# Chunks of four tiles instead of two in the gather-and-scatter ring of a fused graph and mixture kernel

## The chip, the cores and the metric

One core of one Trainium2 chip runs the whole program. The time is the device time of one execution in microseconds; three runs of the kernel before gave a median of 10040.12 us. A profile is one further execution, recorded by the hardware profiler.

## What is computed

Cut to what matters (the dense branches in words):

```python
edge_index = jnp.stack([src, dst])          # 206250 edges, sorted by dst, 6250 nodes, D = 256
xn = layernorm(x)                           # (6250, 256) float32
h = xn
for l in range(3):                          # three relational graph layers, 8 relations
    agg = segment_sum(h[src], edge_type * 6250 + dst).reshape(8, 6250, 256)
    y = einsum('rnd,rde->ne', agg, W[l]) + h @ root[l] + bias[l]
    h = relu(y) if l < 2 else sigmoid(y)
x = x + h + mix(xn)                         # 8 heads of linear attention and a 1024-wide MLP
x = x + moe(layernorm(x))                   # 8 experts, top 2
```

All tensors are float32.

## The kernel before, in words

The order of sum and product is turned round. For each layer, each node's vector is first multiplied with all eight relation matrices and the root matrix; the nine results are a row of a table in HBM (`table[l]`, 56250 rows of 256 floats). The sum over edges is then a gather of table rows and a sum into the node of `dst`. Nodes are taken in 50 **windows** of 125 (`WIN`).

**Phases.** Phase 0 normalises x and fills the first table. Phases 1, 2 and 3 each do a layer's sum window by window, and lay other dense work between two windows: phase 1 the products for the next table and the attention's projections, phase 2 the products for the third table, attention output and MLP, phase 3 router and experts. Between phases all tables must be stored.

**Tiles, chunks, units.** The edges lie in tiles of 128 (`TILE`). `TILES` tiles are a chunk (2 before), `UNIT` chunks are a unit (2, so four tiles), and `RING` chunks (13) are the ring in SBUF, and also a body, the length of the loops on POOL and SP. There are 62 bodies, 806 chunks, 403 units, 1612 tiles. The count of edges is rounded up to whole bodies; pad tiles have index 0 and a target that matches no node. For each window a first and last unit come from a table of bounds that the kernel computes from `dst` (lines 783 to 805). The unit at a window's border is read by both windows; the last window runs to the last unit.

**POOL** (lines 432 to 449): for each chunk it waits until its slot is free (`slots_free`, L443), and issues one indirect DMA a tile (L447): 128 rows of 1 KB from the table, by 128 indices in `idx_now`. Each adds 16 to `gathered[s]`. Twice a body, at slots 0 and `GROUP_A` (7), it waits for the reload of the indices (L441).

**SP** (lines 372 to 382): it waits for each chunk to have landed, in order, adds 1 to `chunks_ready` (L378), and reloads the indices of a group of chunks when all of it has landed (L380).

**DVE** (`onehot_unit`, L842 to L853): for each chunk it waits until the one-hot buffer's last use is over (`onehot_used`, L848), and makes the one-hot matrices of all tiles of the chunk in one instruction (L849): target of the edge against the 125 nodes of the window. There are two buffers, so a one-hot can be made once the matmuls of the chunk before the last are complete. `first_onehots` (L855) makes the first two of the next window ahead.

**PE** (`scatter`, L1151 to L1184): for each chunk it waits for `chunks_ready` and `onehot_ready`, and does one matmul a tile (L1169), which the trace records as two: one-hot (128 x 125) times gathered rows (128 x 256), added up in `ps_out`. The last one of a chunk adds 1 to `onehot_used` on completion. After every unit but a window's first it waits until all units before this one are complete and then frees `UNIT` chunks (L1179, L1180): the slots are freed one unit late, since the border unit is read again. At the window's end L1183 adds the root term and signals `out_done`. ACT then makes `h_win` (L599, L654, L698 in the three phases), PE transposes it (L1108), ACT copies it out (L483), and the products (L1130) follow. In phase 3 PE goes on with the router (L1334) and the experts (L1344, L1355) of the window before.

Of the kernel before, what the change touches and what calls it, by code (L numbers as in the profile page):

```python
# [26 lines left out]
WIN = 125  # L27
WIN_A = 112
TILE = 128
TILES = 2  # L30
RING = 13
UNIT = 2
GROUP_A = 7


def gps_program(nc, t):
# [6 lines left out]
    assert nodes % WIN == 0 and NW % 2 == 0  # L43
    body_edges = TILE * TILES * RING
    BODIES = -(-edges // body_edges)
    CHUNKS = BODIES * RING
    while CHUNKS % UNIT:
        BODIES += 1
        CHUNKS += RING
    UNITS = CHUNKS // UNIT  # L50
    NT = CHUNKS * TILES
    TB = -(-NT // 128)
# [20 lines left out]
    with ExitStack() as ctx:  # L73
        ctx.enter_context(nc.allow_non_contiguous_dma(reason="a few vectors go to a feature a partition"))

        def sb(name, shape, dt=FP32):
            return ctx.enter_context(nc.sbuf_tensor(name, shape, dt))
# [15 lines left out]
        targets = sb("targets", [128, TB * 128])  # L93
        idx_now = sb("idx_now", [128, RING * TILES], U32)
        ring = sb("ring", [128, RING * TILES * D])
        onehot = [sb(f"onehot{i}", [128, TILES, WIN]) for i in range(UNIT)]
        nodes_now = sb("nodes_now", [128, WIN])
# [78 lines left out]
        ordC = edges // SP_  # L176
        assert 3 * ordC <= RING * TILES * D
        order_a = ring[:, 0:ordC].bitcast(I32)
# [154 lines left out]
        def _(sp):  # L333
# [30 lines left out]
            sp.wait_ge(prep_ev, 2 * TB)  # L364
            groups = ((0, GROUP_A), (GROUP_A, RING))
            for g, (s0, s1) in enumerate(groups):
# [22 lines left out]
        def _(pool):  # L389
# [42 lines left out]
            for l in range(3):  # L432
# [3 lines left out]
                with pool.Fori(0, layer_turns) as i:  # L436
                    turn = pool.snap(layer_turns * l + i)
                    for s in range(RING):
                        if s in (0, GROUP_A):

                            pool.wait_ge(idx_loaded[int(s == GROUP_A)], turn * 16 + 16)  # L441

# [961 lines left out]
```

## Time and profile before

| | |
|---|---|
| median of 3 runs | 10040.12 us (10038.99 to 10089.25) |
| profiled execution, span | 10274.9 us |
| its own time beside the span | not recorded; the span is taken for it |
| busy: PE, PE weight load | 6298.0 us (61%), 4307.1 us (42%) |
| busy: POOL, DVE, ACT | 4692.1 us (46%), 2244.8 us (22%), 1095.0 us (11%) |
| DMA | 899.6 MB, mean 88 GB/s |

Engines: PE is TensorE's matmuls, PEld its weight loads, DVE is VectorE, ACT ScalarE, POOL GpSimd, SP SyncE. L849 is line 849 of the kernel. "idle before" is time in which the engine stood still before these instructions; after the arrow stands what ended it. "issue" is a wait that nothing in the profile explains, "remote" and "another core or an unknown queue" one that ended with a semaphore's change to which the profile finds no instruction. PEq and DVEq are the engines' sequencers. The ends of matmuls are modelled from their size, not observed.

### The profile page before, as it was taken

The page shows a single profiled execution, that of the slowest core. Times are in us where ns is not written, and L with a number is a line of the kernel's source. Part 1 is how long each engine was busy: PE and PEld are TensorE (multiplying, and loading weights), DVE is VectorE, ACT ScalarE, POOL GpSimd, SP SyncE. Part 2 cuts the span into 40 slices and gives each one's busy share as a digit, 9 for nine tenths or more (in the row PEclk, how much of TensorE's full clock was granted, in tenths as well). Part 3 has the DMA queues.
Part 4 walks back from the last instruction along what each step waited for, and adds up shares of the span by engine and source line. Part 5 has one row for each costly group of instructions (what it writes and reads, how often), then busy time and mean ns, then how long its engine had stood idle before and what let it go on. Part 6 is the DMA issues. An engine that isn't in the chain of part 4 may idle for free.

```text
span 10274.9 us, 106460 instructions
## 1 busy us (share of the span) xinstructions
PE 6298.0 (61%) x23187; PEld 4307.1 (42%) x23188; DVE 2244.8 (22%) x6475; ACT 1095.0 (11%) x2855; POOL 4692.1 (46%) x4958
## 2 busy tenths in 40 slices
PE   5866556555556666666666665664666665556666
PEld 2333333333333334444444444443444444444445
DVE  2311111111111122222222221222222222222222
ACT  1110000000000000000000000010111111111111
POOL 0134555554555544444444444445444444444443
PEclk9977777777777777777777777777777777777777
DMA  4443333333333333333332323323222222222222
GB/s 120 131 123 95 93 93 98 99 94 93 95 93 96 97 89 89 92 91 91 90 91 87 90 87 93 89 86 97 67 73 67 69 68 71 72 70 69 67 68 60
DMA packets 410721, 899.60 MB, mean 88 GB/s; under 512 B 149828, under 2 KB 236588, under 8 KB 391946
## 3 DMA queue, kind: packets, MB, share of 16 engines
q0 software_dynamic: 232128, 634.17, 21.4%
q10 hardware_dynamic: 116050, 257.82, 8.2%
q1 hardware_dynamic: 62518, 7.30, 0.6%
q8 instruction: 12, 0.20, 0.0%
q14 instruction: 13, 0.11, 0.0%
HBM read 704.42 MB, written 192.01 MB: 87 GB/s over the span
## 4 chain that ended last, share of the span: by engine, by line
PE 38%; issue 29%; another core or an unknown queue 27%; DVE 2%; ACT 2%; ACTq 1%; DVEq 1%; DMA 1%; POOL 0%; POOLq 0%; SPq 0%; PEld 0%; PEldq 0%
PE ps_out L1169 17%; PE ps_y L1130 8%; PE ps_y L1344 3%; PE ps_tr L1286 2%; PE ps_b L1355 2%; PE ps_c L1355 2%; DVE onehot L849 1%; PE ps_tr L1108 0%; PE ps_out L1183 0%; ACT L713 0%; DVEq L849 0%; PE ps_b L1274 0%; PE ps_c L1230 0%; DVEq L885 0%
## 5 line engine op out<-in xcount | busy, mean ns | idle before, releaser
L447 POOL DMA_INDIRECT ring<-table,idx_now x4836 | 4634.1, 958 | 4979.6 <-PEq L1180 3530.7
L1169 PE MATMUL ps_out<-ring,onehot 128*125 x10848 | 3342.2, 461 | 2881.1 <-issue 1772.5
L1169 PEld LDWEIGHTS ps_out<-ring,onehot 128*125 128x125 f32 x10848 | 2290.8, 225 | 3938.9 <-issue 3574.5
L849 DVE TENSOR_TENSOR onehot<-targets,nodes_now 128x250 f32<-128x250 f32 x2712 | 1131.5, 422 | 5341.1 <-remote 2955.1
L1130 PE MATMUL ps_y<-W,hT 128*125 128x512 f32 (+1 forms) x3000 | 1347.1, 600 | 17.5 <-DVE y_stage L739 16.4
L1130 PEld LDWEIGHTS ps_y<-W,hT 128*125 128x125 f32 x3000 | 598.9, 207 | 606.7 <-issue 560.5
L1344 PEld LDWEIGHTS ps_y<-hT,big 128*128 128x128 f32 x3200 | 440.2, 207 | 25.4 <-issue 4.7
L1355 PE MATMUL ps_b<-big,gT 128*125 128x256 f32 x800 | 268.1, 467 | 294.6 <-ACT gT L713 282.2
L1344 PE MATMUL ps_y<-hT,big 128*128 128x125 f32 x3200 | 444.5, 291 | 5.5 <-issue 5.4
L462 ACT COPY y_stage<-ps_y 125x512 f32<-125x512 f32 x450 | 263.5, 585 | 1002.0 <-PE ps_y L1130 973.3
L1286 PE MATMUL ps_tr<-W,gT 128*125 128x256 f32 x800 | 258.2, 493 | 94.6 <-ACT gT L663 94.6
L426 POOL TENSOR_TENSOR rstd<-mv,neg_half 125x1 f32<-125x1 f32 x100 | 54.8, 548 | 554.0 <-DVE mv L822 478.7
L1355 PEld LDWEIGHTS ps_b<-big,gT 128*125 128x125 f32 x800 | 164.3, 229 | 341.8 <-ACT gT L713 291.7
L713 ACT ACTIVATE gT<-ps_y,b1e 128x125 f32<-128x125 f32 x800 | 236.7, 364 | 544.5 <-PE ps_y L1344 343.3
L1286 PEld LDWEIGHTS ps_tr<-W,gT 128*125 128x125 f32 x800 | 196.6, 252 | 165.5 <-ACT gT L663 121.2
L599 ACT ACTIVATE h_win<-ps_out 125x256 f32<-125x256 f32 x50 | 19.2, 383 | 2115.3 <-remote 959.5
L739 DVE COPY y_stage<-ps_y 125x512 f32<-125x512 f32 x150 | 103.7, 691 | 614.4 <-PE ps_y L1130 542.3
L654 ACT ACTIVATE h_win<-ps_out 125x256 f32<-125x256 f32 x50 | 19.2, 383 | 1986.3 <-issue 856.5
L698 ACT ACTIVATE h_win<-ps_out 125x256 f32<-125x256 f32 x50 | 19.2, 383 | 1970.0 <-PE ps_out L1183 941.6
L1355 PE MATMUL ps_c<-big,gT 128*125 128x256 f32 x800 | 200.6, 384 | 0.2 <-ACT gT L713 0.2
L1108 PE MATMUL ps_tr<-ident,h_win 125*128 125x125 f32 x200 | 47.1, 320 | 215.8 <-issue 94.6
L1049 DVE SCALAR_TENSOR_TENSOR acc<-ps_b,combine,acc 125x256 f32<-125x256 f32 x200 | 96.8, 484 | 316.9 <-PE ps_b L1355 313.2
(172 smaller groups left out, 2819.1 us busy)
## 6 DMA issues: line engine op xcount, KB each, us to landing
table<-y_stage ACTq DMA_DIRECT2D x150, 1008.0 KB
ring<-table,idx_now POOLq DMA_INDIRECT x4836
base_in<-table ACTq DMA_DIRECT2D x150, 125.0 KB
table<-y_stage ACTq DMA_DIRECT2D x150, 117.0 KB
x_in<-in_x_dram ACTq DMA_DIRECT2D x100, 125.0 KB
xn_in<-xn_scratch ACTq DMA_DIRECT2D x100, 125.0 KB
xn_scratch<-xn_in ACTq DMA_DIRECT2D x50, 125.0 KB
res_scratch<-res_win ACTq DMA_DIRECT2D x50, 125.0 KB
```

The source lines that it names most:

```text
L426: nc.gpsimd.tensor_tensor(rstd[:, :], mv[:, 1:2], neg_half[:, :], ALU.pow).then_inc(rstd_ready, 1)
L447: nc.gpsimd.indirect_dma_start(ring[:, c * D:(c + 1) * D], None, table[l], bass.IndirectOffsetOnAxis(ap=idx_now[:, c:c + 1], axis=0)).then ...
L462: nc.scalar.copy(y_stage[parity][:, b * 2 * D:(b + 1) * 2 * D], ps_y[BANK[b]][0:WIN, 0:2 * D]).then_inc(y_evac_act, 1)
L713: last = nc.scalar.activation(gT[:, (e % GB) * K + f, :], ps_y[e % 3][:, f * WIN:(f + 1) * WIN], ACT.Gelu, bias=b1e[:, e, f:f + 1])
L739: nc.vector.tensor_copy(y_stage[parity][:, 2 * D:4 * D], ps_y[1][0:WIN, 0:2 * D]).then_inc(y_evac_dve, 1)
L849: nc.vector.tensor_tensor(onehot[u][:, :, :], targets[:, bass.ds(col + u * TILES, TILES)].unsqueeze(2).broadcast_to([128, TILES, WIN]), no ...
L1049: nc.vector.scalar_tensor_tensor(out=acc[parity][:, :], in0=(ps_b, ps_c)[e // 2 % 2][0:WIN, e % 2 * D:(e % 2 + 1) * D], scalar=combine[:, ...
L1130: last = nc.tensor.matmul(ps_y[BANK[b]][0:WIN, 0:n], hT[parity][:, k, :], W[:, k, b * 2 * D:b * 2 * D + n], start=(k == 0), stop=(k == K - 1))
L1169: mm = nc.tensor.matmul(ps_out[0:WIN, 0:D], onehot[u][:, j, :], ring[:, bass.ds(slot + j * D, D)], start=(start and u == 0 and j == 0), st ...
L1286: last = nc.tensor.matmul(ps_tr[0:WIN, 0:D], gT[:, j, :], W2[:, j, :], start=(j == 0), stop=(j == FJ - 1))
L1344: last = nc.tensor.matmul(ps_y[e % 3][:, f * WIN:(f + 1) * WIN], w1e[:, e, k, f * 128:(f + 1) * 128], hT[parity][:, k, :], start=(k == 0), ...
L1355: last = nc.tensor.matmul((ps_b, ps_c)[e // 2 % 2][0:WIN, e % 2 * D:(e % 2 + 1) * D], gT[:, (e % GB) * K + f, :], w2e[:, e, f, :], start=( ...
```

## The change

Four tiles make a chunk and eight a unit; the ring holds six chunks (24 tiles instead of 26), reloaded in two groups of three. All counts that hang on these constants follow: a one-hot instruction makes 128 x 500 elements, a body has 24 tiles, and bodies, chunks, units and pad tiles are counted anew. No other line changes.

```diff
-TILES = 2
-RING = 13
+TILES = 4
+RING = 6
 UNIT = 2
-GROUP_A = 7
+GROUP_A = 3
```

## Rows read from the trace of the kernel before

**Rows 1.** The page: the chain by engine, and two of the costliest groups.
```profile
PE 38%; issue 29%; another core or an unknown queue 27%; DVE 2%; ACT 2%; ACTq 1%; DVEq 1%; DMA 1%; POOL 0%; POOLq 0%; SPq 0%; PEld 0%; PEldq 0%
...
L447 POOL DMA_INDIRECT ring<-table,idx_now x4836 | 4634.1, 958 | 4979.6 <-PEq L1180 3530.7
...
L849 DVE TENSOR_TENSOR onehot<-targets,nodes_now 128x250 f32<-128x250 f32 x2712 | 1131.5, 422 | 5341.1 <-remote 2955.1
```

**Rows 2.** Line L1183 in the three phases: durations, first and last start.
```profile
L1183 PE MATMUL ps_out<-base_in,ident x100: 377/380/451, 710.4 to 3604.8; 125*125 125x256 f32 x100
...
L1183 PE MATMUL ps_out<-base_in,ident x100: 377/381/634, 3717.5 to 6918.8; 125*125 125x256 f32 x100
...
L1183 PE MATMUL ps_out<-base_in,ident x100: 376/381/635, 7014.8 to 10236.4; 125*125 125x256 f32 x100
```

**Rows 3.** Timeline of a window of phase 1: start, duration, what, idle before.
```profile
2022.17 11.01 PE L1169 MATMUL ps_out<-ring,onehot 128*125 x44
...
2026.00 0.95 POOL L447 DMA_INDIRECT ring<-table,idx_now  x1 [12.15 <-PEq L1180]
...
2035.64 0.42 DVE L849 TENSOR_TENSOR onehot<-targets,nodes_now 128x250 f32<-128x250 f32 x1 [3.84 <-remote]
...
2049.90 0.94 POOL L447 DMA_INDIRECT ring<-table,idx_now  x1 [0.30 <-issue]
2054.17 0.42 DVE L849 TENSOR_TENSOR onehot<-targets,nodes_now 128x250 f32<-128x250 f32 x1 [9.54 <-remote]
```

**Rows 4.** The chain in the same window, and into the next: start, duration, what.
```profile
2031.44 3.94 another core or an unknown queue
...
2036.10 7.92 another core or an unknown queue
...
2044.28 9.63 another core or an unknown queue
...
2061.64 0.43 PE ps_out L1183 x2
...
2064.11 0.43 PE ps_tr L1108 x2
...
2080.15 10.66 PE ps_out L1169 x40
```

**Rows 5.** Stretches of 2 us: PE, PEld, DVE, ACT, POOL, PEclk, DMA share, GB/s.
```profile
2018.00:2020.00 2.00, 2.00 (x9) 1.28 (x8) 0.65 (x2) 0.37 (x1) 0.00 (x0) 1.00 0.00 0
...
2052.00:2054.00 2.00, 0.00 (x0) 0.00 (x0) 0.00 (x0) 0.00 (x0) 0.00 (x0) 0.50 0.08 15
```

**Rows 6.** Timeline after that window's scatter, ACT.
```profile
2063.67 0.38 ACT L599 ACTIVATE h_win<-ps_out 125x256 f32<-125x256 f32 x1 [40.72 <-remote]
...
2066.54 0.37 ACT L483 COPY hT<-ps_tr 128x250 f32<-128x250 f32 x1 [2.49 <-remote]
```

**Rows 7.** A window's end in phase 3: first the chain, then the timeline.
```profile
7122.69 13.96 another core or an unknown queue
...
7147.71 0.87 PE ps_c L1355 x4
...
7154.84 1.85 PE ps_out L1169 x8
...
7134.89 0.95 POOL L447 DMA_INDIRECT ring<-table,idx_now  x1 [0.30 <-issue]
...
7138.90 1.39 ACT L713 ACTIVATE gT<-ps_y,b1e 128x125 f32<-128x125 f32 x5 [0.36 <-remote]
```

**Rows 8.** The chain between two scatters of phase 2: first and last piece.
```profile
5214.33 0.43 PE ps_out L1183 x2
...
5235.98 3.45 PE ps_y L1130 x8
```

**Rows 9.** Timeline at the start of the first gathers.
```profile
636.99 1.18 POOL L447 DMA_INDIRECT ring<-table,idx_now  x1 [24.09 <-issue]
...
647.14 0.80 ACT L580 ACTIVATE xhatT<-ps_a,cols 128x125 f32<-128x125 f32 x2 [0.77 <-PE ps_a L1211]
```

## The prediction

> **What bounds the kernel now.** I read the page first. Its chain charges TensorE with 38% of the span, "issue" with 29% and "another core or an unknown queue" with 27% on a one-core program [rows 1]: over half the path is waiting. The gathers (L447) are busy 4634 us and idle 4980 us, mostly until PE frees slots (L1180); they bound nothing on the average. The one-hots (L849) are busy 1132 us. Next, where the time lies: the closing matmul of a window (L1183) comes 50 times a layer, at a mean distance of 59.1, 65.3 and 65.7 us (first to last over 49) [rows 2]. So 9315 of 10275 us are 150 windows of two parts, the scatter (L1169 over about 18 chunks) and the dense work.
>
> Then one window of the first layer. The scatter begins at 2022.17 and does 11 chunks (44 matmul records) in 11.01 us. The POOL had stood still for 12.15 us with the ring full; at 2026.00 slots come free and it gathers without pause, 20 gathers 1.25 us apart, the last at 2049.90 [rows 3]. Six microseconds into this burst the scatter nearly stops: the chain shows waits of 3.94, 7.92 and 9.63 us, each ended by a one-hot, with one chunk between two [rows 4]. The data is not late: between 2018 and 2020 the DMA engines moved 0 GB/s, so the chunks that follow in the ring had landed [rows 5]. The one-hot is not slow: 0.42 us. It starts late, as DVE itself idled 3.84 us until a "remote" event [rows 3], and in the loop DVE waits for one thing, `onehot_used`, which a matmul increments. Those matmuls were recorded long before. My reading: **a PE completion signal, immediate otherwise, is late while a long run of gathers is under way**, by 2 us at first and 8 to 10 us later, and all come through some 3.3 us after the last gather (burst over at 2050.84, next one-hot at 2054.17) [rows 3]. It isn't only the ring's matmuls: L1183 ends at 2062.07 and ACT reads its result at 2063.67, 1.6 us later; the transposes behind it end at 2064.54 and ACT copies at 2066.54 [rows 4, 6]. In layer 3 a chain of such waits lasts 13.96 us, until 7136.65, just after the last gather of that burst (7134.89), and the first gelu follows at 7138.9 [rows 7].
>
> So two cycles meet in a window: PE, free for 10 us, empties the ring; then it stands until the 25 us burst is over.
>
> **The change, part by part.**
> Counts. A body holds 6 x 4 x 128 = 3072 edges; 206250 need 68 bodies, 408 chunks, 204 units, 1632 tiles instead of 1612. A unit is visited once, and once more at each window's border: 204 + 49 = 253 visits of 8 tiles, 2024 a layer instead of 452 x 4 = 1808.
> (1) One-hots: 2712 become 1518, each twice as large. Of 422 ns [rows 1], between the same 422 and double, 844; I take 0.68 us. Beside eight matmuls it is hidden either way; if it weren't, 1518 x 0.68 = 1.03 ms is less than the 1.13 ms now.
> (2) Matmuls: the handshake (one-hot, signal, four matmuls, signal) paces PE at 1.0 us per two tiles [rows 3]. With eight per chunk it should fall back to the bare 0.217 us (four of equal width take 0.87 [rows 7]), 1.73 us for four tiles. A window's 40.5 tiles would need 17.5 us instead of 18.1 for 36.2: the extra tiles are paid by the rhythm. Taken as 0; between -0.6 and +2.2 us a window.
> (3) Prefetch: slots are freed one unit late (the unit at the border is read again). Of 26 tiles in the ring 22 lie ahead of a window's start now; of 24, 16 will.
> (4) SP and POOL: waits, increments and POOL's slot waits halve in number. idx reloads: groups of 12 gathers (15 us) each instead of 14 and 12. Nothing on the path; the 3-chunk group still gives 15 us of cover to a reload.
> (5) Pad tiles: 20 more gathers a layer, all in the last window, which runs to the last unit: 20 x 1.25 = 25 us, 75 us in all. Bound: 0 if hidden.
>
> Now a window, from its first ring matmul. PE does chunks 0 to 3 without waiting; at the fourth's start (5.2 us) it frees the border unit. Now the fourth chunk starts at 3.0 us (11 chunks in 11.01) and POOL's first gather 0.8 later, at 3.83 [rows 3]; so it will be 6.0. The second unit is freed 3.5 us later, the third when chunk 7's data is there: 8 gathers, 6.0 + 7 x 1.25 + 3 = 17.8 us, before the 16 gathers freed so far are spent (26.0). The landing time of 3 us is from the last gather at 2049.90 and traffic that has died down to 15 GB/s by 2052 to 2054 [rows 3, 5]. The fourth unit is freed when chunk 9 can start: its data is there at 6.0 + 15 x 1.25 + 3 = 27.8 us, and it needs chunk 7's completion signal (matmuls done at 20 to 21, late by 4 to 8 us: 24 to 29). Both come before 36.0, the end of the granted gathers. **So the burst does not break**: 1612 / 50 = 32.2 gathers in one run, 40.3 us, over at 46.3. PE's last ring matmul is done at about 32, but its signals stand behind two or three others that pass at 8 to 10 us each; L1183's comes with the end of the burst, 46.3 + 3.3 = 49.6 us.
> From there the dense work runs clear of gathers. Layer 1: from ACT's read at 2063.67 to the next ring matmul at 2080.15 are 16.5 us, less the 2.0 of the late transpose signal: 14.5 [rows 4, 6]. Layer 3: from 7138.9 to 7154.84, 15.9 [rows 7]. Layer 2: 5214.76 to 5239.43 are 24.7 us with late signals inside; between 14.5 and 24.7, I take 19.5, as its up-projection and gelus wait within [rows 8].
> Windows: 64.1, 69.1, 65.5 us against 59.1, 65.3, 65.7: +5.0, +3.8, -0.2, in sum 8.6, x 49 = +421 us. With the pads **+496 us**. The profiled execution spans 10274.9, the median of the runs is 10040.1, 2.3% less; I carry the difference over in microseconds: about 10540 us.
>
> The Trainium skill (SBUF - State Buffer, "SBUF: two separate sides") says that the engines' and the DMA's ports are disjoint and neither can slow the other. By that rule gathers couldn't hold up TensorE's completions; the trace disagrees in its 3.94, 7.92 and 9.63 us waits, unless their cause is another (rival A). The same notes (TensorE: Matmul & The Clock Gate, "The cost: per-tile semaphore tail") price an increment at 26.3 ns; by that alone 1194 fewer would give 31 us, an estimate by that page, and the time would be 10084 with the pads.
>
> **Rivals.**
> A, signals on time (11%): if what makes them late is the number of handshakes, it goes with half of them. Then the scatter is paced by gathers, 32.5 us; windows of 47, 52 and 48.4, -42.7 x 49 + 75: 8025 us. Against: lateness shows on signals of the dense work as well [rows 6, 7].
> B, signals late by some 5 us each, however long the burst (16%): L1183's passes at about 41 us; windows 55.5, 60.5, 56.9: -17.2 x 49 + 75 = -770, 9270 us. This is the case of the **other side**: it decides at chunk 9, and wins if L1183's signal arrives before 46 us on the mean (three windows of h + dense work 14.5, 19.5 and 15.9 against 190.1, less 1.5 for the pads). For: in the run's first burst, begun at 636.99, a transpose signal at 647.1 was not late at all [rows 9]. Against: in the burst shown each wait is longer than the one before it [rows 4].
> C, the burst breaks (14%): if chunk 7's signal comes after 36.0 us, POOL runs dry, signals clear at about 40, and a second short burst covers the dense work as now. h at 43.5: 60, 65.5, and 69.7 in layer 3, whose up-projections wait for the second burst: +5.1 x 49 + 75, 10365 us.
> D, worse (8%): layer 2's dense work keeps its 24.7 us and 16.5 stay in layer 1: 66.5, 74.7, 68: 11050 us.
> E, no change (6%): prefetch lost and rhythm gained cancel. A rival that the change does nothing it says I rule out: all loops take TILES and RING.
>
> **The numbers.** The forecast, 45%, is 10540; its own range is 10350 to 10900. Faster, A and B: 0.27. Within 0.5% (about what a measurement of this kernel can tell): 0.06. Slower, forecast, C and D: 0.67. The range of 9250 to 10900 holds the forecast, B, C and E, 81%.
>
> **What would show it.** POOL: one run of 32 to 40 gathers a window instead of 20 and 12, idle 4.98 ms about as now. L1169: about 0.22 us per matmul while free. ACT at h_win: its idle time up, ended 3 us after the last gather of each burst. L1183 some 32 us after the window's first ring matmul, h_win at 49.6. Distances of L1183 of 64.1, 69.1, 65.5. I am wrong in the reading itself if signals arrive at once in the middle of a 40 us burst, and wrong in size if h_win starts well before the burst's end.

## The result, and the profile after

The kernel after takes 10958.61 us (median of 4 runs, 10948.59 to 10959.58), the kernel before, beside it, 10052.5 us (10038.99 to 10089.25): a ratio of 1.0895, 95% interval 1.0873 to 1.0917. That is 906 us slower; the forecast was 10540 us, and its range ended at 10900.

The page of the kernel after: the span, the chain by engine, and the groups that answer to [rows 1].

```profile
span 10957.3 us, 97403 instructions
...
another core or an unknown queue 57%; PE 22%; issue 13%; ACT 3%; ACTq 2%; PEld 1%; DVE 1%; DMA 1%; POOL 0%; PEldq 0%; DVEq 0%; POOLq 0%; SPq 0%
...
L447 POOL DMA_INDIRECT ring<-table,idx_now x4896 | 4735.5, 967 | 5566.7 <-PEq L1180 4101.7
L1169 PE MATMUL ps_out<-ring,onehot 128*125 x12144 | 3429.5, 444 | 1549.4 <-issue 741.7
...
L849 DVE TENSOR_TENSOR onehot<-targets,nodes_now 128x500 f32<-128x500 f32 x1518 | 1032.6, 683 | 5450.1 <-remote 2178.9
...
L599 ACT ACTIVATE h_win<-ps_out 125x256 f32<-125x256 f32 x50 | 19.2, 383 | 2483.8 <-remote 2135.1
```

No engine has enough new work to explain 906 us: the gathers cost 101 us more, the scatter's matmuls 87 us more for 12% more records, the one-hots 99 us less. What grew is waiting. The share of the chain that no instruction accounts for went from 27% to 57%, and ACT's idle time before `h_win` in the 50 windows of phase 1 is 2484 us, 2135 of them ended by a "remote" event. In the kernel before these two were 2115 and 960 us:

```profile
L599 ACT ACTIVATE h_win<-ps_out 125x256 f32<-125x256 f32 x50 | 19.2, 383 | 2115.3 <-remote 959.5
```

The closing matmul of a window in the three phases, as in [rows 2]:

```profile
L1183 PE MATMUL ps_out<-base_in,ident x100: 377/381/634, 688.6 to 3931.5; 125*125 125x256 f32 x100
...
L1183 PE MATMUL ps_out<-base_in,ident x100: 377/382/634, 4033.0 to 7464.5; 125*125 125x256 f32 x100
...
L1183 PE MATMUL ps_out<-base_in,ident x100: 377/381/634, 7544.2 to 10918.8; 125*125 125x256 f32 x100
```

First to last over 49: 66.2, 70.0 and 68.9 us, against 59.1, 65.3 and 65.7. By the starts in these rows the three times 49 distances sum to 10049 us against 9317, 732 us more. Outside them some 50 us fell away, so the spans differ by 682 us.

One window of phase 1, as in [rows 3]. Timeline: start, duration, what, in brackets the idle time before it.

```profile
2021.94 10.52 PE L1169 MATMUL ps_out<-ring,onehot 128*125 x48
...
2027.96 1.02 POOL L447 DMA_INDIRECT ring<-table,idx_now  x1 [25.37 <-PEq L1180]
...
2037.00 0.75 DVE L849 TENSOR_TENSOR onehot<-targets,nodes_now 128x500 f32<-128x500 f32 x1 [3.59 <-PE ps_out L1169]
...
2043.03 0.68 DVE L849 TENSOR_TENSOR onehot<-targets,nodes_now 128x500 f32<-128x500 f32 x1 [5.28 <-issue]
...
2053.10 1.06 PE L1183 MATMUL ps_out<-base_in,ident 125*125 125x256 f32 x2
...
2057.19 0.68 DVE L849 TENSOR_TENSOR onehot<-targets,nodes_now 128x500 f32<-128x500 f32 x1 [12.52 <-remote]
...
2067.74 0.95 POOL L447 DMA_INDIRECT ring<-table,idx_now  x1 [0.30 <-issue]
2073.34 0.38 ACT L599 ACTIVATE h_win<-ps_out 125x256 f32<-125x256 f32 x1 [50.62 <-remote]
2073.43 0.68 DVE L849 TENSOR_TENSOR onehot<-targets,nodes_now 128x500 f32<-128x500 f32 x1 [15.55 <-remote]
```

POOL restarts 6.02 us after the first ring matmul and issues 32 gathers without a gap, until 2068.69. The closing matmul is over at 2054.16. ACT, which waits for nothing but its signal, starts at 2073.34: **19.2 us after the matmul, and 4.65 us after the end of the last gather's instruction.** The window is no exception: over the 50 windows of each phase `h_win` starts 20.4, 19.1 and 20.5 us behind the matmul in the median (0.75, 0.04 and 0.04 us in the kernel before), and 5.1 us behind the last gather. The chain of the same stretch consists of little else:

```profile
2018.67 3.45 PE ps_y L1130 x8
...
2023.84 49.48 another core or an unknown queue
2073.34 0.39 ACT h_win L599
```

### The profile page after: what moved, and what is told of

Read it like the earlier page. It is cut to its first block, busy times and chain, and to the rows that moved or that the text cites. A ratio compares the mean times of both kernels' runs of the same rounds, so it can differ in the third digit from the quotient of the medians.

```text
span 10957.3 us, 97403 instructions
## 1 busy us (share of the span) xinstructions
PE 6489.4 (59%) x24483; PEld 4714.6 (43%) x24484; DVE 2141.2 (20%) x5281; ACT 1095.9 (10%) x2855; POOL 4793.5 (44%) x5018
## 4 chain that ended last, share of the span: by engine, by line
another core or an unknown queue 57%; PE 22%; issue 13%; ACT 3%; ACTq 2%; PEld 1%; DVE 1%; DMA 1%; POOL 0%; PEldq 0%; DVEq 0%; POOLq 0%; SPq 0%
PE ps_y L1130 7%; PE ps_out L1169 3%; PE ps_y L1344 2%; PE ps_b L1355 2%; PE ps_c L1355 2%; PE ps_tr L1286 1%; PE ps_b L1274 1%; PE ps_c L1274 1%; PEld ps_out L1169 1%; ACTq L472 1%; PE ps_tr L1108 1%; ACT L713 1%; ACT y_stage L462 0%; ACTq L669 0%
## 5 line engine op out<-in xcount | busy, mean ns | idle before, releaser
L447 POOL DMA_INDIRECT ring<-table,idx_now x4896 | 4735.5, 967 | 5566.7 <-PEq L1180 4101.7
L1169 PE MATMUL ps_out<-ring,onehot 128*125 x12144 | 3429.5, 444 | 1549.4 <-issue 741.7
L1169 PEld LDWEIGHTS ps_out<-ring,onehot 128*125 128x125 f32 x12144 | 2611.0, 220 | 2363.6 <-issue 1917.3
L849 DVE TENSOR_TENSOR onehot<-targets,nodes_now 128x500 f32<-128x500 f32 x1518 | 1032.6, 683 | 5450.1 <-remote 2178.9
L1108 PE MATMUL ps_tr<-ident,h_win 125*128 125x125 f32 x200 | 65.5, 428 | 1695.0 <-ACT h_win L599 840.7
L1344 PE MATMUL ps_y<-hT,big 128*128 128x125 f32 x3200 | 516.1, 299 | 576.0 <-issue 575.5
L1108 PEld LDWEIGHTS ps_tr<-ident,h_win 125*128 125x128 f32 x200 | 28.1, 198 | 1745.9 <-ACT h_win L599 864.1
L1344 PEld LDWEIGHTS ps_y<-hT,big 128*128 128x128 f32 x3200 | 485.5, 215 | 599.0 <-issue 578.0
L599 ACT ACTIVATE h_win<-ps_out 125x256 f32<-125x256 f32 x50 | 19.2, 383 | 2483.8 <-remote 2135.1
L654 ACT ACTIVATE h_win<-ps_out 125x256 f32<-125x256 f32 x50 | 19.2, 383 | 2331.8 <-remote 2053.6
L698 ACT ACTIVATE h_win<-ps_out 125x256 f32<-125x256 f32 x50 | 19.2, 383 | 2319.8 <-remote 2046.6
L1286 PE MATMUL ps_tr<-W,gT 128*125 128x256 f32 x800 | 194.6, 397 | 27.7 <-ACT gT L663 27.7
```

What stands on the lines that cost most here:

```text
L447: nc.gpsimd.indirect_dma_start(ring[:, c * D:(c + 1) * D], None, table[l], bass.IndirectOffsetOnAxis(ap=idx_now[:, c:c + 1], axis=0)).then ...
L849: nc.vector.tensor_tensor(onehot[u][:, :, :], targets[:, bass.ds(col + u * TILES, TILES)].unsqueeze(2).broadcast_to([128, TILES, WIN]), no ...
L1108: last = nc.tensor.transpose(ps_tr[:, k * WIN:(k + 1) * WIN], src[:, k * 128:(k + 1) * 128], ident[0:WIN, 0:WIN])
L1169: mm = nc.tensor.matmul(ps_out[0:WIN, 0:D], onehot[u][:, j, :], ring[:, bass.ds(slot + j * D, D)], start=(start and u == 0 and j == 0), st ...
L1286: last = nc.tensor.matmul(ps_tr[0:WIN, 0:D], gT[:, j, :], W2[:, j, :], start=(j == 0), stop=(j == FJ - 1))
L1344: last = nc.tensor.matmul(ps_y[e % 3][:, f * WIN:(f + 1) * WIN], w1e[:, e, k, f * 128:(f + 1) * 128], hT[parity][:, k, :], start=(k == 0), ...
```

## The experiments

All are compared with the kernel before on the same chip. Each of the five sets ran on another chip, and these turned out to be of two kinds. (No chip was used for two sets, so whether the kind belongs to the chip or to its state at that time was not seen; the chip of the result and that of the profile of the kernel before are not recorded.) On three (sets 1, 4 and 5) the kernel before took 10047 to 10228 us, as in the result above; on two (sets 2 and 3) it took 6879 and 6876 us. I call the first kind "holding", the second "prompt", for what their traces show of PE's signals. The expectations of sets 1 and 2 were written when only the holding kind was known. "Theory G" in them is the prediction's mechanism: PE's completion signals are held back as long as a run of gathers lasts.

### Set 1, holding (before 10082.0 us): which part of the change, and two rivals to the cause

**Unit of eight tiles alone, chunks of two.**

```diff
-RING = 13
-UNIT = 2
-GROUP_A = 7
+RING = 12
+UNIT = 4
+GROUP_A = 6
```

> The change with its unit but not its chunk: TILES 2, UNIT 4, RING 12, GROUP_A 6, so chunks of two tiles, units of eight, 24 tiles in the ring, four one-hot buffers. Theory G (completion signals of PE are late while a run of gathers lasts, and eight-tile releases let the run last until all gathers of a window are done): as slow as the change, runs of 32 gathers, h_win some 5 us after a run's end, 10850 to 11050 us. Rival S (what counts is how many signals there are per tile): twice the change's signals, so the run breaks or the scatter stops as in the kernel before, 10000 to 10400 us.

Measured 10246.25 us, ratio 1.017 (1.0134 to 1.0207), in rival S's range and not in theory G's. In its trace most runs of gathers break after 24, and `h_win` starts some 44 us into the window.

**Chunk of four alone, unit of one chunk (four tiles), and so a single one-hot buffer.**

```diff
-TILES = 2
-RING = 13
-UNIT = 2
-GROUP_A = 7
+TILES = 4
+RING = 6
+UNIT = 1
+GROUP_A = 3
```

> The change with its chunk but not its unit: TILES 4, UNIT 1, RING 6, so one signal and one one-hot per four tiles, and slots freed by four tiles; there is one one-hot buffer only, so PE pauses about 1 us at each chunk. Theory G: the run of gathers breaks again in most windows, because a late signal holds back the next release sooner; between 9900 and 10600 us. Rival S: halving the signals is what cost the time, so 10900 us or more.

Measured 10504.05 us, ratio 1.0426 (1.0375 to 1.0476); runs again break, mostly after 20 to 24. This lies in theory G's range and not in S's. So neither half makes the 906 us, and neither theory foresaw both results. My reading, which no run tests by itself: only both together leave few enough signals, each worth enough tiles, for a run to last all 32 gathers.

**A shallow queue of gathers.** From the third slot of the ring on POOL waits until the chunk before the last has landed, so that at most two chunks, four gathers, are under way.

```diff
                         apart(pool)
+                        if s >= 2:
+                            pool.wait_ge(gathered[s - 2], (turn + 1) * (16 * TILES))
+                            apart(pool)
```

> The kernel before, but POOL waits before a chunk's gathers until the chunk before the last has landed (not for the first two slots of a body), so at most four gathers are under way or queued, without a pause between gathers. Theory G: it is the run of gathers itself that makes signals late; same time within 1%, waits of 4, 8 and 10 us in each window as before. Rival Q (signals are late while gathers are queued up on POOL, and the granted ones are dispatched far ahead): signals on time, scatter at the rate of gathers, 7300 to 8600 us.

Measured 10055.94 us, ratio 0.9977 (0.9954 to 1.0). The wait leaves nine in ten gathers without a gap (4401 of 4835 follow within 0.35 us, 4504 in the kernel before), and the time stays: it is not the depth of POOL's queue.

**No reads of the ring.** The scatter multiplies with a constant tile (the sum over edges is left out).

```diff
-                                                  ring[:, bass.ds(slot + j * D, D)],
+                                                  Wx[:, 0, :],
```

> The kernel before, but the scatter's matmuls read a constant tile (part of Wx) in place of the gathered rows, so the sum over edges is left out; all waits, gathers and signals stay. Theory G: signals as late as before, 9900 to 10200 us. Rival R (a matmul that reads the ring while gathers write into it is slow or acknowledged late): signals on time, 7300 to 8600 us.

Measured 10091.71 us, in one run, where the kernel before took 10031 to 10106. Reading what the gathers write is not the cause either.

### Set 2, prompt (before 6879.12 us)

**The kernel after, a gap once in 24 gathers.** POOL lets the chunk before land first, at slot 3 of 6.

```diff
                         apart(pool)
+                        if s in (3,):
+                            pool.wait_ge(gathered[s - 1], (turn + 1) * (16 * TILES))
+                            apart(pool)
```

> The kernel after, with one wait more on POOL: before the fourth chunk of each ring turn it waits for the third chunk to land, so that a run of gathers can hold 24 at most and has a gap of some 3 us behind it. Theory G (PE's completion signals are held back while a run of gathers lasts, and come at its end): the run breaks after at most 24 gathers instead of 32, h_win comes at some 44 us of the window instead of 51.3, and the time is 10100 to 10450 us, near the 10246 of chunks of two tiles with units of eight, although chunk size, unit and ring are those of the kernel after. Rival S (the time goes by the size of chunk and unit itself: waits for four one-hots at once, a ring of six): 10850 to 11150 us, since the extra waits can only cost. What tells: the trace's runs of gathers by length, and h_win's start after the window's first matmul.

**The same at slots 1, 3 and 5: runs of 8.**

> The kernel after, with such a wait before the second, fourth and sixth chunk of each ring turn: runs of 8 gathers (10 us), each with a gap of some 3 us behind it. Theory G: no signal is held longer than about 8 us, the scatter ends early (20 to 30 us of the window) and h_win starts within 5 us of it; POOL itself then needs 32 x 1.25 + 4 x 3 = 52 us a window, so the time is 8300 to 9600 us, below both kernels. Rival P (POOL becomes the bound: each gap costs more than 3 us, or work of the dense part is held back just as much): 10000 to 10900 us. Rival S: 11000 us or more.

**The kernel before, a quarter of each row's bytes** (sum over edges left out).

```diff
-                                ring[:, c * D:(c + 1) * D], None, table[l],
+                                ring[:, c * D:c * D + D // 4], None, table[l].rearrange("n (q d) -> (n q) d", q=4),
```

> The kernel before, where each gather brings a quarter of each row's bytes and the scatter reads a constant tile in place of the ring (the sum over edges is left out). The number of gathers, rows and waits is unchanged. Theory V (it is the bytes written to SBUF that hold the signals back): with a quarter of them the signals come on time and the time falls to 8000 to 9300 us. Theory N (it is the gathers themselves, their number and their rows, whatever bytes they bring): 10000 to 10120 us, no change from the 10082 us of the same kernel with full rows.

**The kernel after, each window's last release put off** until PE has `h_win` or the tanh.

```diff
                 unit(first, True)
-                    with pe.Fori(first + 1, last + 1) as pos:
+                    with pe.Fori(first + 1, last) as pos:
...
+                    n = unit(last, False)
+                    pe.wait_ge(onehot_used, n + UNIT)
...
+                    def release():
+                        apart(pe)
+                        with pe.If(last > start):
+                            pe.sem_inc(slots_free, UNIT)
```

> The kernel after, where PE releases the last two chunks of each window's scatter not when their matmuls are done but after it has h_win (layers 1 and 2) or the tanh (layer 3). Theory G: POOL runs out of free slots about 4 to 8 gathers earlier, so the run ends at some 36 to 41 us of the window instead of 46.2, the held signals come 5 us behind that, and h_win starts at 41 to 46 us instead of 51.3; the remaining gathers run beside the dense part. 147 windows x 5 to 8 us earlier, less what the later gathers cost the next scatter: 9900 to 10500 us. Rival L (the gathers put off are late for the next window, whose scatter waits for them): 10800 to 11300 us, with the gap moved from h_win to the first matmuls of the ring.

Measured, in this order: 8369.28 us, ratio 1.216 (1.214 to 1.218); 8925.08 us, 1.2976 (1.2955 to 1.2998); 6860.73 us, 0.9976 (0.9966 to 0.9986); 8130.96 us, 1.1815 (1.1795 to 1.1835). The second lies in theory G's range and the third speaks, by its number, for bytes as the cause. But the kernel before itself took 6879 us, and in all four traces `h_win` starts 0.04 us behind the closing matmul whatever the gathers do. So the set says nothing on what holds signals back; only the comparison beside each number kept this from becoming a false proof. The last edit was tried here alone (45 us slower than the kernel after on the other prompt chip); on a holding chip it wasn't tried.

### Set 3, prompt again (before 6875.69 us): what the change costs where no signal is late

> The kernel after itself, beside the kernel before. In the last set of runs the kernel before took 6879 us instead of 10050, and no completion signal of PE was late in any of four kernels (h_win 0.04 us behind the scatter's last matmul). Where the kernel before takes 6879 us, theory C (with signals on time the kernel before is bound by POOL's gathers, 41 us a window, and the change takes that away: a ring released 8 tiles at a time starves POOL): the kernel after takes 8000 to 8300 us (ratio 1.16 to 1.21), 47 to 51 us a window, h_win 0.04 us behind the scatter. Rival (the change is nearly free there, and the deferred release was what cost): 6900 to 7200 us. Where the kernel before takes 10050 us: 10900 to 11000 us again, ratio 1.08 to 1.10.

Measured 8086.43 us, ratio **1.176** (1.1739 to 1.1781). The window that answers to the one above:

```profile
2002.67 2.74 PE L1169 MATMUL ps_out<-ring,onehot 128*125 x8 [3.18 <-SPq L378]
...
2015.83 1.06 PE L1183 MATMUL ps_out<-base_in,ident 125*125 125x256 f32 x2
...
2016.93 0.38 ACT L599 ACTIVATE h_win<-ps_out 125x256 f32<-125x256 f32 x1 [31.60 <-PE ps_out L1183]
...
2030.99 10.52 PE L1169 MATMUL ps_out<-ring,onehot 128*125 x48
...
2036.91 1.12 POOL L447 DMA_INDIRECT ring<-table,idx_now  x1 [5.45 <-PEq L1180]
```

The same instructions at the same pace (first stretch of 48 records again 10.52 us), but `h_win` comes 0.04 us after the matmul instead of 19.2, while gathers are under way. The dense part ends at 2030.99, and POOL stands still for 5.45 us at the start of the window, until the border unit is read again and freed (over the whole run such a gap is 7.3 us in the median, once a window). The kernel before has no trace of its own on such a chip. In its trace with a quarter of the bytes that gap isn't there: it goes on at the pace of its gathers through the window's border, and so is bound by POOL:

```profile
1536.76 0.94 POOL L447 DMA_INDIRECT ring<-table,idx_now  x1 [0.30 <-issue]
...
1537.29 0.68 PE L1183 MATMUL ps_out<-base_in,ident 125*125 125x256 f32 x2
1538.01 0.94 POOL L447 DMA_INDIRECT ring<-table,idx_now  x1 [0.30 <-issue]
1538.01 0.38 ACT L599 ACTIVATE h_win<-ps_out 125x256 f32<-125x256 f32 x1 [23.45 <-PE ps_out L1183]
```

**Unit of eight, chunks of two, again.**

> Chunks of two tiles, units of four chunks (8 tiles), a ring of twelve. Where the kernel before takes 6879 us: theory C says that the unit of 8 tiles is what starves POOL, so this takes most of the loss, 7900 to 8300 us; a rival says that the ring of six big chunks does it (a gather waits for a whole slot of four tiles), and this takes 6900 to 7300 us. Where the kernel before takes 10050 us: 10200 to 10300 us again.

Measured 7808.98 us, ratio 1.1362 (1.1343 to 1.1381), a little below the first theory's range and far above the rival's. 933 of the 1211 us come with the unit, its ring of 24 tiles and its 20 pad tiles a layer, 277 with the larger chunk.

> The kernel after with a gap of some 3 us behind every 8 gathers. Where the kernel before takes 10050 us: theory G (PE's signals are held back while a run of gathers lasts) 8900 to 9600 us, below both kernels, h_win within 5 us of the scatter's last matmul; rival P (dense part or gaps cost as much): 10000 us or more. Where it takes 6879 us: 8900 to 8950 us again.

Measured 8920.83 us: on a prompt chip gaps only cost, 834 us here.

> The kernel before with a quarter of each gathered row's bytes and a constant in place of the ring (the sum over edges is left out). Where the kernel before takes 10050 us: theory V (the bytes written hold the signals back) 6850 to 8000 us; theory N (the number of gathers and rows does) 10000 to 10120 us. Where it takes 6879 us: 6850 to 6870 us again, bound by 4836 gathers at 1.27 us.

Measured 6861.21 us.

### Set 4, holding (before 10046.55 us): the run of gathers is what holds the signals

**The kernel before with gaps.** Runs of 8 to 10 gathers, then POOL waits for the last chunk to land.

```diff
                         apart(pool)
+                        if s in (4, 8, 12):
+                            pool.wait_ge(gathered[s - 1], (turn + 1) * (16 * TILES))
+                            apart(pool)
```

> The kernel before with a wait on POOL for the chunk before to land, at three of the 13 slots of the ring: runs of 8 to 10 gathers, each with a gap of some 3 us. Where the kernel before takes 10050 us: theory G (the run of gathers holds the signals back, a gap lets them go) 8000 to 9500 us, ratio under 0.95; rival H (signals are late for another reason, and the gaps only cost) 10100 to 11500 us. Where it takes 6877 us, bound by gathers: 41 us a window plus 3.6 gaps of 3 us is 52 us, so 8200 to 8600 us, ratio 1.19 to 1.25, by every theory.

Measured **8476.84 us, ratio 0.8442** (0.8423 to 0.8462). Three waits on POOL, which add no work and take none away, make the kernel 16% faster. Its lines stand 3 lower: L1186 is L1183, L602 is L599, L852 is L849, L450 is L447. First its page:

```profile
PE 34%; issue 29%; another core or an unknown queue 16%; POOL 8%; DMA 6%; DVE 3%; ACT 2%; ACTq 1%; DVEq 1%; POOLq 0%; PEld 0%; PEldq 0%; SPq 0%
...
L450 POOL DMA_INDIRECT ring<-table,idx_now x4836 | 4640.9, 960 | 3175.5 <-issue 1588.7
```

Then the timeline of one window:

```profile
1715.65 1.12 POOL L450 DMA_INDIRECT ring<-table,idx_now  x1 [0.30 <-issue]
...
1718.64 0.42 DVE L852 TENSOR_TENSOR onehot<-targets,nodes_now 128x250 f32<-128x250 f32 x1 [2.69 <-PE ps_out L1172]
...
1721.95 0.95 POOL L450 DMA_INDIRECT ring<-table,idx_now  x1 [5.18 <-DMA ring<-table,idx_now]
...
1748.04 0.60 PE L1186 MATMUL ps_out<-base_in,ident 125*125 125x256 f32 x2
1748.67 0.38 ACT L602 ACTIVATE h_win<-ps_out 125x256 f32<-125x256 f32 x1 [34.04 <-PE ps_out L1186]
1749.28 0.95 POOL L450 DMA_INDIRECT ring<-table,idx_now  x1 [2.50 <-DMA ring<-table,idx_now]
```

The gathers cost what they cost before (4641 us against 4634), POOL is idle 1804 us less, and `h_win` is prompt in 49 of 50 windows of phase 1. It isn't everywhere: in phases 2 and 3 it is late in 14 and 20 of 50 windows, by up to 5.9 us. The held share of the chain falls from 27% to 16%.

**Chunk of four, unit of four, again.**

> Chunks of four tiles, a unit of one chunk (four tiles), a ring of six. Where the kernel before takes 6877 us: the window's scatter touches 36 tiles instead of 40, 12 gathers behind POOL's restart instead of 16, so it ends some 5 us earlier than in the kernel after (27 instead of 32 us) and the dense part of 14 to 18 us follows: 41 to 46 us a window, and 7000 to 7500 us. Rival (the chunk of four itself starves POOL as much as the unit): 7800 us or more. Where it takes 10050 us: 10400 to 10600 us again.

Measured 10497.45 us, ratio 1.0452 (1.0429 to 1.0474). How the chunk of four alone does on a prompt chip was not seen.

**A quarter of the bytes, now where signals are held.**

> As before: a quarter of each row's bytes, the sum over edges left out. Where the kernel before takes 10050 us: bytes theory 6850 to 8000 us, number theory 10000 to 10120 us. Where it takes 6877 us: 6860 us again.

Measured 10061.57 us, in one run, where the kernel before took 10019 to 10060. The chain by engine on its page, and then the chain in order of time in one window:

```profile
PE 39%; issue 31%; another core or an unknown queue 23%; DVE 2%; ACT 2%; ACTq 1%; DVEq 1%; DMA 0%; POOL 0%; POOLq 0%; SPq 0%; PEld 0%
```

```profile
1908.73 6.30 another core or an unknown queue
1915.28 8.84 another core or an unknown queue
1924.85 8.40 another core or an unknown queue
```

A quarter of the bytes moves nothing: what holds the signals goes with the gather instructions and their rows by number, not with what they write. Which of the two it is, POOL's instructions or the rows on their way, no run separates.

### Set 5, holding (before 10227.85 us): how the cost goes with the length of the run

The kernel after was not run on this chip; its 10958.61 us are from the result.

> The kernel after with a gap behind every 8 gathers. Where the kernel before takes 10050 us: theory G says that the hold goes, so the time is near the 8920 us that this kernel takes where no signal is late, 8900 to 9300 us, some 1800 us under the kernel after; a theory by which chunk and unit size cost the 906 us by themselves gives 10000 us or more. Where the kernel before takes 6877 us: 8920 us a third time.

Measured 9429.98 us, ratio 0.9224 (0.9201 to 0.9248). 130 us above the range: in phases 2 and 3 the dense part still takes 22 us where it takes 18 and 15 on a prompt chip.

> The kernel after with one gap for each 24 gathers. Where the kernel before takes 10050 us, theory G: runs of 12 to 24 gathers in place of 32, h_win at 30 to 45 us of the window instead of 51.3, 9000 to 10500 us, between the runs of 8 and the unbroken 32. A theory without the run's length: 10900 us or more. Where the kernel before takes 6877 us: 8370 us again.

Measured 10799.48 us, ratio 1.0565 (1.0538 to 1.0592): above theory G's range, and just under the other's. The group of `h_win` in phase 1, on its page and on that of the kernel with runs of 8:

```profile
L602 ACT ACTIVATE h_win<-ps_out 125x256 f32<-125x256 f32 x50 | 19.2, 384 | 2203.9 <-remote 1381.7
```

```profile
L602 ACT ACTIVATE h_win<-ps_out 125x256 f32<-125x256 f32 x50 | 19.2, 384 | 1891.7 <-PE ps_out L1186 1891.7
```

The first of the two is the kernel with runs up to 24. With runs of 8, none of ACT's waiting in phase 1 ends with a "remote" event any more; with runs up to 24, 1382 us of it do.

**The kernel before, gaps at two slots: runs of 12 to 14.**

```diff
+                        if s in (6, 12):
```

> The kernel before with gaps at two of the 13 slots: runs of 12 to 14 gathers. POOL's own bound is 41 us + 2.5 x 2.6 us = 47.5 us a window (7650 us in all); signals can be held up to 12 x 1.25 = 15 us. Where the kernel before takes 10050 us: 8000 to 9300 us; below 8477 if POOL's bound decides, above it if the hold does. Where it takes 6877 us: 7600 to 8000 us, bound by POOL.

Measured 9475.9 us, ratio 0.9264 (0.924 to 0.9288), 176 us above the range: longer runs are held longer, and that costs more than the gaps they save. In its trace `h_win` comes 4.9 us behind the closing matmul in the median window of phase 1, by up to 12.6, and most of ACT's waiting for it ends with a "remote" event:

```profile
L602 ACT ACTIVATE h_win<-ps_out 125x256 f32<-125x256 f32 x50 | 19.2, 383 | 1643.6 <-remote 1238.2
```

Runs of 8 to 10 were the best tried. Shorter ones were not.

All kernels on both kinds of chip, medians in us:

| kernel | longest run of gathers | holding | prompt | difference |
|---|---|---|---|---|
| before (bytes cut to a quarter) | holding mostly 20 to 24, prompt unbroken | 10062 | 6861 | 3200 |
| before, whole | holding the same, prompt not traced | 10047 to 10228 | 6876, 6879 | 3170 to 3350 |
| after | 32 | 10959 | 8086 | 2872 |
| unit of eight, chunk of two | holding mostly 24, prompt 32 | 10246 | 7809 | 2437 |
| after, runs up to 24 | 24 | 10799 | 8369 | 2430 |
| after, runs of 8 | 8 | 9430 | 8921, 8925 | 505 to 509 |
| before, runs of 8 to 10 | 10 | 8477 | not run | |

## Why the prediction was wrong

The direction and the mechanism were right, and most times in the window; the size was not: 496 us forecast, 906 measured. Two steps failed above all. The excess of the profile's span over the median was carried over in microseconds, which is 224 of the 410 us missing. And the dense part of a window, put at 14.5, 19.5 and 15.9 us, took 15.7, 19.7 and 18.1, which is 176 us. A later `h_win` (76 us) and the first and last windows (60 us) add to it, and 125 us come off again, as shown below.

**The burst.** Forecast: POOL begins at 6.0 us, does not break, is over at 46.3. Measured: 6.0 and 46.2 to 46.8 us, one run of 32 gathers in 135 of some 150 windows. The argument that the fourth unit would be freed before the granted gathers were spent held. **The counts** held too: 1518 one-hots of 0.683 us against 0.68, 12144 matmul records (three layers of 2024, each recorded as two), the bare rhythm of 0.22 us, the closing matmul at 31.2 us in the window shown (30.2 in the median) where I said 32. That the prefetch falls to 16 tiles is seen in the restart at 6 us.

**"L1183's comes with the end of the burst, 46.3 + 3.3 = 49.6 us": right in kind, short in size.** `h_win` starts at 51.3 us in the median window of phase 1, 4.65 us behind the last gather in the window shown. I had taken 3.3 us from a one-hot of the kernel before, behind a run of 20 gathers; behind a run of 32 it is more. On the mean of all windows, prompt ones included, `h_win` comes at 50.5, 50.0 and 50.5 us.

**"From there the dense work runs clear of gathers": right, but not at full pace.** The way from `h_win` to the next ring matmul takes 15.7, 19.7 and 18.1 us on the mean, against my 14.5, 19.5 and 15.9. On a prompt chip the same three are 14.4, 18.3 and 15.4. Part of the difference is TensorE's clock: PE had stood still for 19 us, and the stretches after it show a granted clock of 0.50 until 2082, the lower of its two levels (1.2 of 2.4 GHz); the prompt kernel, whose rest was shorter, was granted 0.93, 0.64 and 0.79 in its first 9 us. The two transposes (L1108) take 0.68 us at the lower level and 0.44 in the prompt kernel. How much of the difference the clock makes wasn't measured by itself. Stretches as in [rows 5], first the kernel after, then the same kernel on the prompt chip:

```profile
2073.00:2076.00 3.00, 0.68 (x2) 0.29 (x2) 0.68 (x1) 1.02 (x3) 0.00 (x0) 0.50 0.05 3
...
2079.00:2082.00 3.00, 3.00 (x5) 1.01 (x4) 0.69 (x1) 0.00 (x0) 0.00 (x0) 0.50 0.00 0
2082.00:2090.00 8.00, 8.00 (x33) 5.14 (x32) 0.65 (x2) 2.75 (x6) 0.00 (x0) 0.99 0.00 0
```

```profile
2017.00:2020.00 3.00, 0.70 (x4) 0.47 (x5) 0.00 (x0) 1.28 (x3) 2.39 (x3) 0.93 0.31 87
2020.00:2023.00 3.00, 3.00 (x7) 1.39 (x6) 0.14 (x1) 0.80 (x2) 2.09 (x3) 0.64 0.58 191
2023.00:2026.00 3.00, 3.00 (x12) 1.56 (x11) 0.56 (x1) 0.59 (x1) 2.39 (x3) 0.79 0.35 97
```

I had read the dense part's length from windows where the engine had not just rested so long, and left the clock out of the sum. A part of it was in my 14.5 us unseen: in the window of [rows 3] the granted clock was 0.50 and 0.58 from 2067 to 2073.

**The pads, "75 us in all": the price was near, the comparison was not.** The last window of a phase runs to the last unit. In phase 1 its closing matmul comes 93.8 us after the one before; in the kernel before it was 45.1 us:

```profile
3837.46 1.06 PE L1183 MATMUL ps_out<-base_in,ident 125*125 125x256 f32 x2
...
3931.25 0.60 PE L1183 MATMUL ps_out<-base_in,ident 125*125 125x256 f32 x2
```

```profile
3559.52 0.60 PE L1183 MATMUL ps_out<-base_in,ident 125*125 125x256 f32 x2
...
3604.62 0.60 PE L1183 MATMUL ps_out<-base_in,ident 125*125 125x256 f32 x2
```

With the other two phases, 99.3 against 48.4 and 98.2 against 52.3, that makes 145 us. The last windows of the kernel after are 28 to 31 us longer than its others, on the holding and on the prompt chip alike, some 88 us for the 75 I had priced. What I had overlooked is the other side: in the kernel before the last windows are 14 to 17 us shorter than its others. Their last run is of 10 gathers only, as nothing is left to gather for a next window.

**"I carry the difference over in microseconds": this alone is 224 of the 410 us missing.** The profiled execution of the kernel before spans 222 us more than its median; that of the kernel after spans 10957.3 us beside a median of 10958.6. The excess belongs to that execution or to its chip, which isn't recorded (in set 5 the kernel before took 10228 us); it is no fixed difference between a span and a time. The windows of the queue experiment, which is as fast as the kernel before, sum to 9099 us in its profile, those of [rows 2] to 9317. The spans compared, the change costs 682 us, and 186 us are left for the three points above: 311 us more in the windows (732 against 421 us, pads included in the 732), less the 75 us that I had put outside, less 50 us that fell away between the phases. Of the 311 the later `h_win` makes 76, the slower dense part 176 and the scatters of the first and last windows 60.

**The rivals.** A's condition, signals on time, was realised by a chip, not by the number of handshakes: there its time, 8025 us from windows of 47, 52 and 48.4 us, met a measured 8086 us from distances of 46.7, 51.5 and 48.8 us. The three rows of that run:

```profile
L1183 PE MATMUL ps_out<-base_in,ident x100: 376/382/635, 684.7 to 2972.7; 125*125 125x256 f32 x100
...
L1183 PE MATMUL ps_out<-base_in,ident x100: 377/616/635, 3061.8 to 5584.5; 125*125 125x256 f32 x100
...
L1183 PE MATMUL ps_out<-base_in,ident x100: 376/494/635, 5658.4 to 8051.7; 125*125 125x256 f32 x100
```

The arithmetic of the window was sound; that the totals meet so well is luck in part, since A's sum too had the 235 us of the profile taken off. And I compared it with the time of a kernel that was held. Where nothing is held the kernel before is at 6877 us, and A would have been the worst case for the change, not the best. B and C fell with the unbroken burst: the closing matmul's signal came some 20 us late in the median, not 5, and only 12 runs ended after 24. D came nearest in time (11050 us), for other reasons than it gave; its windows of 66.5 and 74.7 us are also 0.4 us more than 49.6 and its own 16.5 and 24.7. The Trainium skill (SBUF - State Buffer, "SBUF: two separate sides") says that a DMA cannot be slowed by a compute operation nor the other way round. On the prompt chips the trace agrees, with 0.04 us from matmul to `h_win` in the midst of gathers; on the holding ones it doesn't, with 19.2 us. That a quarter of the bytes changed nothing fits the page in one thing: whatever holds the signals, it is not the amount of data on its way into SBUF.

**What stays open.** Why signals were held on three chips and not on two, and whether they always are. The trace records the delay, not its place. The Trainium skill (Perfetto Trace Analysis, "Tensor Engine Instruction (MATMUL, LD_WEIGHTS)") says that a matmul's end in the profile is estimated, and that the signal goes out only when PSUM has acknowledged the write. So by the rows alone a late matmul and a late signal look alike. No run here shows a matmul's true end. One thing speaks for the signal: in the window shown PE starts another chunk's matmuls at 2050.43 and the closing one at 2053.10, at their usual pace, while the one-hot that waits for the chunk begun at 2045.13 starts only at 2057.19.

## What to carry to other kernels

A change that saves signals and waits can cost time when those waits also broke up a long run of gathers. Look in the trace for consumers that start only when such a run ends, and try a gap in the run before anything else: here a wait on POOL at every eighth to tenth gather was worth 16% on a chip that holds signals. But measure the kernel before on the same chip each time. On a prompt chip it runs at 6877 us, gaps only cost there (the kernel after went from 8086 to 8921 us), and of the versions tried the kernel before is the fastest there.

When a ring is freed unit by unit, the border unit is read twice: its size is taken from the prefetch and added to the scatter. Where no signal was held, a unit of eight instead of four tiles, with a ring of 24 tiles instead of 26, cost 14%. And a profile's span is compared with another profile's span; what it exceeds the median by isn't carried over.

## What the runs showed of the hardware

- The same kernel takes 10050 us on some chips and 6877 us on others, a factor of 1.46. The two profiles of the kernel after have 97403 instructions each, and the gather's instruction has 967 ns on the mean in the one and 973 ns in the other.
- On the slower ones TensorE's completion signals come up to 21 us late (kernel after) while gathers are issued every 1.25 us. With gaps of some 2.5 us behind every 8 to 10 gathers the worst is 5.9 us. The gathers' number matters, their bytes don't (one run, 10062 us).
- In the windows shown the delay did not begin at a fixed age of the run. In the kernel before signals are late from its sixth microsecond on, in the kernel after the chunks up to 20 us into the window, 14 us into the run, are on time.
